# Expert down projection: both weight parts in one 512-column matmul, halves added on the way out of PSUM

## The chip, the cores and the metric

The kernel runs on one core of a Trainium2 chip. The metric is the device time of one execution in microseconds; smaller is better. Three runs of the kernel before gave 782.05, 783.87 and 785.30 us. The trace is that of one further execution with the hardware profiler on.

## The reference

One transformer layer: a layer norm modulated by a vector c, causal attention with 16 heads over 2048 tokens of width 256, and a mixture of 8 experts. The part that the change touches is the experts:

```python
C = _capacity(T, E)                      # 320 slots for each of E = 8 experts
...
dispatch_data = jnp.einsum('tec,th->ech', sec_mask_f, tokens)
h = jnp.einsum('ech,ehi->eci', dispatch_data, wi)        # 320 x 256 by 256 x 1024
h = jax.nn.gelu(h, approximate=False)
expert_out = jnp.einsum('eci,eih->ech', h, wo)           # 320 x 1024 by 1024 x 256
ans = jnp.einsum('tec,ech->th', combine_weights, expert_out)
...
x = x + gb * _L0_ffn_ref(h, ...)
```

Each token goes to one expert at most, so the result row of a slot is the token's row of x plus gb times its gate probability times the expert's row.

## The kernel before

Attention comes first and takes some 600 us; then tokens are ranked, scattered into slot rows in HBM (`slot_rows`, 320 for each expert, each with the row of x, the normalised row, the probability and the token's number) and read back by expert into `slots_sb`. The change touches only the expert stage behind that.

**Tiles.** An expert's 320 slots are CT3 = 3 row tiles of 128, 128 and 64 rows. Its inner width of 1024 is cut into IT = 8 tiles of 128. The engines walk through n = 0 to 63 (expert e = n // 8, inner tile it = n % 8).

**Split numbers.** Matmuls take 4-byte operands in the format fp32r, which keeps fewer bits than float32. To keep the precision every operand is held as a high part (rounded) and a low part (the rest): `w_split[e % 2][:, 0]` and `[:, 1]` for the weights, `acts[:, n % 3, 0]` and `[:, 1]` for the activations. A product is made of three terms, low x high, high x low and high x high (PAIRS, L1401).

**TensorE** (L1439 to L1448). `up(n)` makes six matmuls of 320 columns into bank n % 3 (L1413). At the first inner tile of an expert, `turn_slots` transposes the next expert's slots (L1396). Then `down_to(n - 2)` makes, for each of the three row tiles, three matmuls of 256 columns (L1430): the activations are the stationary operand, the weights stream, and the result adds up over the eight inner tiles in columns 0 to 255 of the bank of that row tile (banks 3, 4, 5; each holds 512 columns of float32). So down_to of an expert's last inner tile runs behind up of the next expert's second one, and the next expert's first down_to waits for `down_read` of each row tile, the mark that DVE has read the bank (L1428).

**ACT** waits for `up_done`, makes Gelu twice, once rounded into acts (L862) and once in full into act_raw (L865), and in between casts the next expert's weights (L837, inner tiles 2 to 5) and turns its slots (L843, inner tile 0).

**DVE** makes the low part of acts (L1139), the low part of the next expert's weights (L1098) and slots (L1106, L1109). At the second inner tile of an expert it calls `finish_rows` for the one before: for each row tile bank times probability times the gate row (L1120). `add_rows` adds the token's row of x (L1127), one row tile at the second, one at the seventh and one at the eighth inner tile. Behind the last expert both run at once for all three.

**POOL** waits for each row tile (L730) and scatters it to `out` by an indirect DMA (L731). The instructions of each engine run in order. `link` on POOL (L645) gives an instruction a mark and makes the engine's next instruction wait for it.

**SP** loads the weights and slots of later experts; slots of expert e reuse those of e - 4 once their rows are stored (L628).

Of the kernel before, what the change touches and what calls it, by code (L numbers as in the profile page):

```python
# [21 lines left out]
F32 = mybir.dt.float32  # L22
# [4 lines left out]
ALU = mybir.AluOpType  # L27
ACT = mybir.ActivationFunctionType
AX = mybir.AxisListType

P = 128
D = 256
# [17 lines left out]
E = 8  # L50
I = 1024
IT = I // P
# [3 lines left out]
CT3 = -(-CAP // P)  # L56
CAPW = CT3 * P
LAST_ROWS = CAP - (CT3 - 1) * P
BIAS_FROM = (NG - 2) * NB
DOWN_LAG = 2  # L60
TAIL_TILES = (NB - 1) * TB
# [214 lines left out]
def layer(nc, x, w_qk, b_qk, w_v, w_o, b_rows, w_gate, w_in, w_down, c_col, w_mod, out):  # L276
# [13 lines left out]
    with ExitStack() as ctx:  # L290
        def sem(name):
            return ctx.enter_context(nc.semaphore(name))

        def sb(name, shape, dt):
            return ctx.enter_context(nc.sbuf_tensor(name, shape, dt))
# [5 lines left out]
        DOWN_BANKS, SLOT_BANKS = (3, 4, 5), (6, 7)  # L301
# [83 lines left out]
        SR = 4  # L385
# [4 lines left out]
        AR = 3  # L390
        acts = sb("acts", [P, AR, 2, CAPW], F32R)
        down = sb("down", [P, 2, CT3, D], F32)


        loaded_c = sem("loaded_c")
# [79 lines left out]
        act_used = sem("act_used")  # L475
        down_done = sem("down_done")
        down_read = sem("down_read")
        rows_ready = sem("rows_ready")
        kept_stored = sem("kept_stored")
        rows_stored = [sem(f"rows_stored{r}") for r in range(2)]  # L480
# [48 lines left out]
        def rows_of(st):  # L529
            return min(P, CAP - st * P)  # L530
# [111 lines left out]
        def _(pool):  # L642
# [84 lines left out]
            for e in range(E):  # L727
                for st in range(CT3):
                    rows = rows_of(st)
                    pool.wait_ge(rows_ready, CT3 * e + st + 1)  # L730
                    pool.indirect_dma_start(  # L731
                        out=out, out_offset=bass.IndirectOffsetOnAxis(
                            ap=slots_sb[0:rows, e % SR, st, ROW - 1:ROW].bitcast(U32), axis=0),
                        in_=down[0:rows, e % 2, st, :], in_offset=None, bounds_check=S - 1, oob_is_err=False)\
                        .then_inc(rows_stored[e % 2], 16)
# [4 lines left out]
        def _(act):  # L740
# [98 lines left out]
            def split_slots(e):  # L839

                for ft in range(DT):
                    act.wait_ge(slots_turned, e * DT + ft + 1)
                    act.activation(slotT[:, e % 2, 0, ft, :], bank[SLOT_BANKS[ft]][:, 0:CAP], ACT.Identity,  # L843
                                   bias=mod_col[:, 2, ft:ft + 1], scale=mod_col[:, 3, ft:ft + 1]).then_inc(slotT_high, 1)


            act.activation(c_tmp[0:1, 2, 0:1], c_tmp[0:1, 0, 0:1], ACT.Gelu)

            act.wait_ge(max_scored, units_before[-1])
# [3 lines left out]
            for n in range(E * IT):  # L853
                e, it = divmod(n, IT)
                act.wait_ge(up_done, n + 1)
                if n >= AR:

                    m = n - AR
                    act.wait_ge(act_used, (IT - 1) * (m // IT) + min(m % IT + 1, IT - 1))
                    if m % IT == IT - 1:  # L860
                        act.wait_ge(down_done, CT3 * (m // IT + 1))
                act.activation(acts[:, n % AR, 0, 0:CAP], bank[n % 3][:, 0:CAP], ACT.Gelu)  # L862
                if n >= 2:
                    act.wait_ge(act_ready, n - 1)
                act.activation(act_raw[:, n % 2, :], bank[n % 3][:, 0:CAP], ACT.Gelu).then_inc(gelu_done, 1)  # L865
                if e + 1 < E and 2 <= it < 2 + CH:
                    split_weights(e + 1, it - 2)
                if e + 1 < E and it == 0:
                    split_slots(e + 1)

        @block.vector
        def _(dve):
# [239 lines left out]
            def finish_rows(e):  # L1112

                if e >= 2:
                    dve.wait_ge(rows_stored[e % 2], 16 * CT3 * (e // 2))
                for st in range(CT3):
                    k = CT3 * e + st
                    r = slice(0, rows_of(st))
                    dve.wait_ge(down_done, k + 1)
                    dve.scalar_tensor_tensor(out=down[r, e % 2, st, :], in0=bank[DOWN_BANKS[st]][r, 0:D],  # L1120
                                             scalar=slots_sb[r, e % SR, st, 2 * D:2 * D + 1], in1=gates[r, 1, :],
                                             op0=ALU.mult, op1=ALU.mult).then_inc(down_read, 1)

            def add_rows(e, st):
                r = slice(0, rows_of(st))
                dve.wait_ge(down_read, CT3 * e + st + 1)
                dve.tensor_tensor(down[r, e % 2, st, :], down[r, e % 2, st, :], slots_sb[r, e % SR, st, 0:D],  # L1127
                                  ALU.add).then_inc(rows_ready, 1)

            ADD_AT = (DOWN_LAG - 1, IT - 2, IT - 1)  # L1130
            dve.memset(acts[:, :, :, CAP:CAPW].bitcast(F32), 0.0).then_inc(pads_zeroed, 1)
            for c in range(CH):
                split_weights(0, c)
# [2 lines left out]
            for n in range(E * IT):  # L1136
                e, it = divmod(n, IT)
                dve.wait_ge(gelu_done, n + 1)
                dve.tensor_tensor(acts[:, n % AR, 1, 0:CAP], act_raw[:, n % 2, :], acts[:, n % AR, 0, 0:CAP].bitcast(F32),  # L1139
                                  ALU.subtract).then_inc(act_ready, 1)  # L1140
                if it == DOWN_LAG - 1 and e >= 1:
                    finish_rows(e - 1)
                if it in ADD_AT and e >= 1:
                    add_rows(e - 1, ADD_AT.index(it))
                if e + 1 < E:
                    if 2 <= it < 2 + CH:
                        split_weights(e + 1, it - 2)
                    if it in (0, IT - 2):
                        split_slots(e + 1, 0 if it == 0 else 1)
            finish_rows(E - 1)  # L1150
            for st in range(CT3):
                add_rows(E - 1, st)

        @block.tensor
        def _(pe):
# [262 lines left out]
            def down_to(n):  # L1418
                e, it = divmod(n, IT)
                if it == 0:  # L1420
                    pe.wait_ge(w_ready, CH * (e + 1))
                if n == 0:
                    pe.wait_ge(pads_zeroed, 1)
                pe.wait_ge(act_ready, n + 1)
                col = DT * I + it * D
                for st in range(CT3):
                    if it == 0 and e >= 1:
                        pe.wait_ge(down_read, CT3 * (e - 1) + st + 1)  # L1428
                    for i, (a, b) in enumerate(PAIRS):
                        mm = pe.matmul(bank[DOWN_BANKS[st]][:, 0:D], acts[:, n % AR, a, st * P:(st + 1) * P],  # L1430
                                       w_split[e % 2][:, b, col:col + D], start=(it == 0 and i == 0),
                                       stop=(it == IT - 1 and i == len(PAIRS) - 1))
                    if it == IT - 1:
                        mm.then_inc(down_done, 1)
                if it < IT - 1:
                    mm.then_inc(act_used, 1)
# [45 lines left out]
```

## Time and profile before

| | |
|---|---|
| Three runs, us | 782.05, 783.87 (median), 785.30 |
| Span of the profiled execution, us | 782.6 |
| Instructions | 12208 |
| PE busy | 689.1 us, 88% |
| PE weight loads busy | 367.2 us, 47% |
| DVE busy | 561.1 us, 72% |
| ACT busy | 459.5 us, 59% |
| POOL busy | 133.9 us, 17% |
| Mean granted TensorE clock | 0.943 of 2.4 GHz |

The shares are means over the whole span, and the attention has other limits than the experts. PE's busy time overlaps: a matmul's record covers its way through the array as well, so the distance from one start to the next tells what it costs, not its own duration. "Idle before" in a row is the time that the engine stood still ahead of that instruction, with what released it.

### The profile page before, as it was taken

The numbers are of one execution on the slowest core, as the hardware profiler recorded it, in microseconds if no ns is written. First come the engines' busy times: TensorE is split into PE (matmuls) and PEld (weight loads), VectorE is DVE, ScalarE is ACT, GpSimd is POOL, SyncE is SP. The second block draws the span as 40 slices with busy tenths as digits, with TensorE's granted clock in tenths as the row PEclk, the third lists the DMA queues.
The fourth block names the chain that finished last, engine by engine and source line by source line (L and its number), as shares of the span: only waits on it lengthen the run. The fifth ranks groups of instructions, "written<-read, shape, count | busy, mean of one in ns | idle before, by whom it ended". The sixth has DMA issues, their size and how long they took to land.

```text
span 782.6 us, 12208 instructions
## 1 busy us (share of the span) xinstructions
PE 689.1 (88%) x4290; PEld 367.2 (47%) x4290; DVE 561.1 (72%) x1467; ACT 459.5 (59%) x962; POOL 133.9 (17%) x194
## 2 busy tenths in 40 slices
PE   4686989999999998999999999989996279999994
PEld 3564534432323343323332323242543269999994
DVE  7754778788888787988888898960435437777762
ACT  1422445566676667766677676657783336656551
POOL 6000222220001132003310201100105300121122
PEclk9869889999999999999999999999999559999998
DMA  7436126630006033005900006000004283455200
GB/s 243 109 76 144 41 57 147 162 68 14 2 0 162 1 81 81 2 1 124 308 1 1 1 1 214 1 28 1 28 28 162 90 234 115 155 182 201 92 23 17
DMA packets 42111, 66.53 MB, mean 85 GB/s; under 512 B 3822, under 2 KB 31985, under 8 KB 41466
## 3 DMA queue, kind: packets, MB, share of 16 engines
q1 hardware_dynamic: 39746, 59.44, 27.3%
q0 software_dynamic: 2304, 6.31, 2.2%
q8 instruction: 34, 0.56, 0.3%
q14 instruction: 27, 0.22, 0.1%
HBM read 39.36 MB, written 26.78 MB: 85 GB/s over the span
## 4 chain that ended last, share of the span: by engine, by line
PE 74%; DVE 10%; ACT 8%; issue 4%; DMA 2%; POOL 1%; SPq 0%; DVEq 0%; POOLq 0%; ACTq 0%
PE bank L1245 17%; PE bank L1295 15%; PE bank L1325 14%; PE bank L1430 9%; PE bank L1413 8%; ACT probs L802 4%; PE bank L1187 3%; DVE chunk_max L1049 2%; PE bank L1350 2%; PE bank L1216 1%; PE bank L1396 1%; ACT qk_sb L751 1%; PE bank L1373 1%; PE bank L1228 1%; DVE stats L907 1%
## 5 line engine op out<-in xcount | busy, mean ns | idle before, releaser
L802 ACT ACTIVATE probs<-bank 128x512 f32<-128x512 f32 (+3 forms) x640 | 298.3, 537 | 124.1 <-PE bank L1325 123.0
L1049 DVE TENSOR_REDUCE chunk_max<-bank 128x1 f32<-128x512 f32 x384 | 250.7, 685 | 36.9 <-PE bank L1295 35.9
L1325 PE MATMUL bank<-stacks 104*128 104x512 bf16 (+3 forms) x640 | 195.4, 356 | 13.5 <-ACT probs L802 10.1
L1295 PE MATMUL bank<-stacks 96*128 96x512 bf16 (+3 forms) x640 | 197.7, 359 | 7.9 <-DVE chunk_max L1049 3.2
L1245 PE MATMUL bank<-probs,v_sb 128*32 128x512 f32 (+3 forms) x1280 | 151.6, 546 | 0.1
L1055 DVE CUSTOM_DVE_ANT_0 masked<-bank,causal 128x128 bf16<-128x128 f32 (+3 forms) x256 | 120.7, 484 | 15.4 <-PE bank L1295 14.6
L1295 PEld LDWEIGHTS bank<-stacks 96*128 96x128 bf16 x640 | 56.0, 98 | 160.0 <-DVE chunk_max L1049 79.4
L698 POOL TENSOR_SCALAR_AFFINE_SELECT probs<-probs 128x512 f32<-128x512 f32 x64 | 40.6, 635 | 397.4 <-ACT probs L802 397.4
L1325 PEld LDWEIGHTS bank<-stacks 104*128 104x128 bf16 x640 | 62.2, 100 | 98.7 <-ACT probs L802 65.6
L1430 PE MATMUL bank<-w_split,acts 128*128 128x256 f32 x576 | 79.9, 284 | 0.0
L1430 PEld LDWEIGHTS bank<-w_split,acts 128*128 128x128 f32 x576 | 74.5, 190 | 1.5 <-issue 0.8
L1413 PE MATMUL bank<-slotT,w_split 128*128 128x320 f32 x384 | 70.0, 320 | 2.1 <-DVE slotT L1109 2.1
L1413 PEld LDWEIGHTS bank<-slotT,w_split 128*128 128x128 f32 x384 | 59.5, 196 | 3.1 <-issue 2.3
L862 ACT ACTIVATE acts<-bank 128x320 fp32r<-128x320 f32 x64 | 28.0, 438 | 55.4 <-PE bank L1413 55.4
L1139 DVE TENSOR_TENSOR acts<-act_raw,acts 128x320 fp32r<-128x320 f32 x64 | 31.4, 490 | 33.6 <-ACT act_raw L865 33.6
L1187 PEld LDWEIGHTS bank<-hT,w_qk_sb 128*128 128x128 f32 x256 | 40.7, 219 | 13.8 <-issue 9.1
L1098 DVE TENSOR_TENSOR w_split<-w_raw,w_split 128x1024 fp32r<-128x1024 f32 x32 | 38.9, 1224 | 10.6 <-ACT w_split L837 10.6
L731 POOL DMA_INDIRECT out<-down,slots_sb x24 | 23.6, 984 | 132.0 <-DVE down L1127 127.2
L1187 PE MATMUL bank<-hT,w_qk_sb 128*128 128x128 f32 x256 | 43.7, 309 | 2.7 <-ACT hT L771 2.7
L1245 PEld LDWEIGHTS bank<-probs,v_sb 128*32 128x32 f32 x1280 | 25.4, 108 | 44.0 <-issue 27.6
L751 ACT ACTIVATE qk_sb<-bank,b_qk_sb,qk_scale 128x512 f32<-128x512 f32 x16 | 12.4, 777 | 43.2 <-PE bank L1187 43.2
L837 ACT CAST w_split<-w_raw 128x1024 fp32r<-128x1024 f32 x32 | 33.3, 1049 | 0.0
(140 smaller groups left out, 533.6 us busy)
## 6 DMA issues: line engine op xcount, KB each, us to landing
stacks<-qk_rows SPq DMA_DIRECT2D x6, 1536.0 KB, 12.4
w_raw<-w_in SPq DMA_DIRECT2D x8, 1024.0 KB, 5.0
w_raw<-w_down SPq DMA_DIRECT2D x8, 1024.0 KB, 8.0
qk_rows<-part SPq DMA_DIRECT2D x32, 192.0 KB, 2.9
slot_rows<-empty SPq DMA_DIRECT2D x1, 5140.0 KB, 28.9
slots_sb<-slot_rows SPq DMA_DIRECT2D x8, 514.0 KB, 4.0
qk_rows<-part SPq DMA_DIRECT2D x32, 128.0 KB, 2.4
stacks<-qk_rows SPq DMA_DIRECT2D x8, 384.0 KB, 4.5
```

Of the source, the lines that this page charges most:

```text
L698: pool.affine_select(out=d, in_=d, compare_op=ALU.is_ge, fill=0.0, base=0, pattern=[[0, HG], [1, P]], channel_multiplier=-1).then_inc(diag ...
L802: act.activation(probs[:, s % 3, h, 0:width], bank[SCORE_BANKS[u % 3]][:, 0:width], ACT.Exp)\
L837: act.copy(chunk(w_split[e % 2][:, 0, :], c), chunk(w_raw[:, e % 2, :], c)).then_inc(w_high, 1)
L1049: dve.tensor_reduce(to, src[:, 0:QB], AX.X, ALU.max).then_inc(max_read, 1)
L1055: dve.tensor_tensor_reduce(out=masked[:, u % 3, 0:width], in0=src[:, 0:width], in1=causal[:, QB - width:QB], scale=1.0, scalar=NEG, op0=AL ...
L1098: dve.tensor_tensor(chunk(w_split[e % 2][:, 1, :], c), chunk(w_raw[:, e % 2, :], c), chunk(w_split[e % 2][:, 0, :], c).bitcast(F32), ALU.s ...
L1187: mm = pe.matmul(bank[MISC_BANK][:, at:at + width], w_qk_sb[:, k, g * P:(g + 1) * P], hT[:, k, b * QB + at:b * QB + at + width], start=(k ...
L1245: mm = pe.matmul(bank[VALUE_BANK][CT * h:CT * (h + 1), lo:QB], v_sb[:, kt, g * HG + h, :], probs[:, s % 3, h, 0:QB - lo], start=first, sto ...
L1295: pe.matmul(bank[MAX_BANKS[u % 3]][:, 0:width], stack(g, 0)[0:KR, h, q0:q0 + P], stack(g, 1)[0:KR, h, c * QB:c * QB + width], start=True, ...
L1325: pe.matmul(bank[SCORE_BANKS[u % 3]][:, 0:QB - lo], stack(g, 1)[0:KR + MR, h, kt * P:(kt + 1) * P], stack(g, 0)[0:KR + MR, h, b * QB + lo: ...
L1413: mm = pe.matmul(bank[n % 3][:, 0:CAP], w_split[e % 2][:, a, col:col + P], slotT[:, e % 2, b, k, :], start=(i == 0 and k == 0), stop=(i == ...
L1430: mm = pe.matmul(bank[DOWN_BANKS[st]][:, 0:D], acts[:, n % AR, a, st * P:(st + 1) * P], w_split[e % 2][:, b, col:col + D], start=(it == 0 ...
```

## The change

In `down_to` the high activations now stream the high and the low weights as one matmul of 512 columns: its result fills the whole bank, high x high in columns 0 to 255 and high x low in 256 to 511. The second matmul, low activations by high weights, adds to columns 256 to 511. The last row tile uses 66 stationary columns, not 128. The two halves of a bank must now be added. ACT does the first step in a new function `scale_low`: columns 256 to 511 times probability into `low_part`. It stands behind the Gelus of the second inner tile, and behind the loop for the last expert. DVE's `finish_rows` waits for it and makes columns 0 to 255 times probability plus low_part. The gate product that this displaces becomes the former `add_rows`, now `gate_rows`, and the addition of x's row moves to POOL, in front of each scatter, through `link`.

```diff
+LAST_COLS = LAST_ROWS + 2
...
+        low_part = sb("low_part", [P, CT3, D], F32)
...
                     pool.wait_ge(rows_ready, CT3 * e + st + 1)
+                    link(pool.tensor_tensor(down[0:rows, e % 2, st, :], down[0:rows, e % 2, st, :],
+                                            slots_sb[0:rows, e % SR, st, 0:D], ALU.add))
                     pool.indirect_dma_start(
...
+            def scale_low(e):
+
+                for st in range(CT3):
+                    k = CT3 * e + st
+                    r = slice(0, rows_of(st))
+                    act.wait_ge(down_done, k + 1)
+                    if e >= 1:
+                        act.wait_ge(down_read, k + 1 - CT3)
+                    act.activation(low_part[r, st, :], bank[DOWN_BANKS[st]][r, D:2 * D], ACT.Copy,
+                                   scale=slots_sb[r, e % SR, st, 2 * D:2 * D + 1]).then_inc(low_scaled, 1)
...
+                if it == DOWN_LAG - 1 and e >= 1:
+                    scale_low(e - 1)
                 if e + 1 < E and 2 <= it < 2 + CH:
                     split_weights(e + 1, it - 2)
...
+            scale_low(E - 1)
...
-                    dve.wait_ge(down_done, k + 1)
+                    dve.wait_ge(low_scaled, k + 1)
                     dve.scalar_tensor_tensor(out=down[r, e % 2, st, :], in0=bank[DOWN_BANKS[st]][r, 0:D],
-                                             scalar=slots_sb[r, e % SR, st, 2 * D:2 * D + 1], in1=gates[r, 1, :],
-                                             op0=ALU.mult, op1=ALU.mult).then_inc(down_read, 1)
-
-            def add_rows(e, st):
+                                             scalar=slots_sb[r, e % SR, st, 2 * D:2 * D + 1], in1=low_part[r, st, :],
+                                             op0=ALU.mult, op1=ALU.add).then_inc(down_read, 1)
+
+            def gate_rows(e, st):
...
-                dve.tensor_tensor(down[r, e % 2, st, :], down[r, e % 2, st, :], slots_sb[r, e % SR, st, 0:D],
-                                  ALU.add).then_inc(rows_ready, 1)
+                dve.tensor_tensor(down[r, e % 2, st, :], down[r, e % 2, st, :], gates[r, 1, :],
+                                  ALU.mult).then_inc(rows_ready, 1)
...
-                    for i, (a, b) in enumerate(PAIRS):
-                        mm = pe.matmul(bank[DOWN_BANKS[st]][:, 0:D], acts[:, n % AR, a, st * P:(st + 1) * P],
-                                       w_split[e % 2][:, b, col:col + D], start=(it == 0 and i == 0),
-                                       stop=(it == IT - 1 and i == len(PAIRS) - 1))
+                    at = st * P
+                    cols = P if st < CT3 - 1 else LAST_COLS
+                    out = bank[DOWN_BANKS[st]][0:cols, :]
+
+                    pe.matmul(out.rearrange("p (a d) -> p a d", a=2), acts[:, n % AR, 0, at:at + cols],
+                              w_split[e % 2][:, :, col:col + D], start=it == 0, stop=True, skip_group_check=True)
+                    mm = pe.matmul(out[:, D:2 * D], acts[:, n % AR, 1, at:at + cols],
+                                   w_split[e % 2][:, 0, col:col + D], start=False, stop=True, skip_group_check=True)
```

## Rows read from the trace of the kernel before

**Rows 1.** The page: busy tenths in 40 slices of 19.6 us, TensorE and its granted clock

```profile
PE   4686989999999998999999999989996279999994
...
PEclk9869889999999999999999999999999559999998
```

**Rows 2.** Busy time by stretch: length, then PE, PEld, DVE, ACT, POOL, clock, DMA

```profile
645.00:772.00 127.00, 127.00 (x948) 122.31 (x947) 88.77 (x156) 76.39 (x158) 20.14 (x21) 1.00 0.37 119
```

**Rows 3.** The chain that ended last, in the expert stage: start, us, what

```profile
704.23 0.99 PE bank L1396 x6
...
707.38 1.06 PE bank L1430 x9
708.45 0.89 PE bank L1413 x6
```

**Rows 4.** Waits from 640 to 783 us: in total, times, the longest

```profile
POOL out L731 <- DVE down L1127: 127.2, 16, 37.8
ACT acts L862 <- PE bank L1413: 50.7, 62, 1.4
```

**Rows 5.** Timeline of the end: start, us, what [idle before <-releaser]

```profile
769.10 3.33 PE L1430 MATMUL bank<-w_split,acts 128*128 128x256 f32 x27
...
770.51 0.41 DVE L1127 TENSOR_TENSOR down<-down,slots_sb 64x256 f32<-64x256 f32 x1
771.71 0.91 POOL L731 DMA_INDIRECT out<-down,slots_sb  x1 [0.96 <-DVE down L1127]
771.84 1.26 DVE L1120 SCALAR_TENSOR_TENSOR down<-bank,slots_sb,gates 128x256 f32<-128x256 f32 x3 [0.92 <-PE bank L1430]
773.02 1.08 DVE L1127 TENSOR_TENSOR down<-down,slots_sb 128x256 f32<-128x256 f32 x3
774.22 0.97 POOL L731 DMA_INDIRECT out<-down,slots_sb  x1 [1.60 <-DVE down L1127]
775.50 0.97 POOL L731 DMA_INDIRECT out<-down,slots_sb  x1 [0.31 <-issue]
776.78 0.91 POOL L731 DMA_INDIRECT out<-down,slots_sb  x1 [0.30 <-issue]
```

**Rows 6.** Groups by line from 600 us on: count | busy us, mean ns | idle before

```profile
L1430 PE MATMUL bank<-w_split,acts 128*128 128x256 f32 x576 | 79.9, 284 | 0.0
L1430 PEld LDWEIGHTS bank<-w_split,acts 128*128 128x128 f32 x576 | 74.5, 190 | 1.5 <-issue 0.8
...
L824 ACT COPY rest<-bank 128x256 f32<-128x256 f32 x4 | 1.5, 372 | 8.7 <-PE bank L1361 8.7
...
L847 ACT ACT_TABLE_LOAD x1 | 1.3, 1283 | 0.0
```

**Rows 7.** The chain at the stage's start, with the clock still at 1.2 GHz

```profile
640.34 1.92 PE bank L1430 x9
```

**Rows 8.** Timeline of PE in the attention: start, us, what

```profile
299.81 0.38 PE L1325 MATMUL bank<-stacks 104*128 104x512 bf16 x1
300.02 0.33 PE L1295 MATMUL bank<-stacks 96*128 96x384 bf16 x1
...
301.02 0.39 PE L1325 MATMUL bank<-stacks 104*128 104x512 bf16 x1
301.34 1.07 PE L1245 MATMUL bank<-probs,v_sb 128*32 128x512 f32 x8
```

**Rows 9.** Timelines of ACT and of DVE at an expert's boundary

```profile
707.75 0.43 ACT L865 ACTIVATE act_raw<-bank 128x320 f32<-128x320 f32 x1
709.37 0.44 ACT L862 ACTIVATE acts<-bank 128x320 fp32r<-128x320 f32 x1 [1.18 <-PE bank L1413]
709.70 0.43 ACT L865 ACTIVATE act_raw<-bank 128x320 f32<-128x320 f32 x1
...
708.63 1.25 DVE L1120 SCALAR_TENSOR_TENSOR down<-bank,slots_sb,gates 128x256 f32<-128x256 f32 x3
```

**Rows 10.** POOL's additions in the attention stage: ns min/median/max

```profile
L711 POOL TENSOR_TENSOR token<-token,product x16: 635/687/747, 367.6 to 447.0; 128x256 f32<-128x256 f32 x16
```

More of the change, by code:

```diff
@@ L477, in layer @@
         down_read = sem("down_read")
+        low_scaled = sem("low_scaled")
         rows_ready = sem("rows_ready")
@@ L1118, in finish_rows @@
                     r = slice(0, rows_of(st))
-                    dve.wait_ge(down_done, k + 1)
+                    dve.wait_ge(low_scaled, k + 1)
                     dve.scalar_tensor_tensor(out=down[r, e % 2, st, :], in0=bank[DOWN_BANKS[st]][r, 0:D],
-                                             scalar=slots_sb[r, e % SR, st, 2 * D:2 * D + 1], in1=gates[r, 1, :],
-                                             op0=ALU.mult, op1=ALU.mult).then_inc(down_read, 1)
-            def add_rows(e, st):
+                                             scalar=slots_sb[r, e % SR, st, 2 * D:2 * D + 1], in1=low_part[r, st, :],
+                                             op0=ALU.mult, op1=ALU.add).then_inc(down_read, 1)
+            def gate_rows(e, st):
                 r = slice(0, rows_of(st))
                 dve.wait_ge(down_read, CT3 * e + st + 1)
-                dve.tensor_tensor(down[r, e % 2, st, :], down[r, e % 2, st, :], slots_sb[r, e % SR, st, 0:D],
-                                  ALU.add).then_inc(rows_ready, 1)
-            ADD_AT = (DOWN_LAG - 1, IT - 2, IT - 1)
+                dve.tensor_tensor(down[r, e % 2, st, :], down[r, e % 2, st, :], gates[r, 1, :],
+                                  ALU.mult).then_inc(rows_ready, 1)
+            GATE_AT = (DOWN_LAG - 1, IT - 2, IT - 1)
             dve.memset(acts[:, :, :, CAP:CAPW].bitcast(F32), 0.0).then_inc(pads_zeroed, 1)
@@ L1142, in _ @@
                     finish_rows(e - 1)
-                if it in ADD_AT and e >= 1:
-                    add_rows(e - 1, ADD_AT.index(it))
+                if it in GATE_AT and e >= 1:
+                    gate_rows(e - 1, GATE_AT.index(it))
                 if e + 1 < E:
@@ L1151, in _ @@
             for st in range(CT3):
-                add_rows(E - 1, st)
+                gate_rows(E - 1, st)
         @block.tensor
```

## The prediction

> **What bounds the kernel now.** I read the page first: its slices show TensorE at nine tenths or more in six of the last eight, with the granted clock at nine tenths in seven of them [rows 1]. The expert stage is this last sixth of the span, and only it holds changed code, so I asked for the busy time of each engine in that stretch [rows 2]: from 645 to 772 us PE is busy for all of 127 us at a granted clock of 1.00 (2.4 GHz), DVE for 88.8, ACT for 76.4, POOL for 20.1. Then the chain that ended last, inside the stage [rows 3]: it alternates between L1430 (9 matmuls in 1.06 us) and L1413 (6 in 0.89 us), with nearly 60 such pieces of each in the stage, and nothing else stands between them except 6 transposes for each expert. So the stage lasts as long as TensorE's stream. The waits say the same from the other side [rows 4]: ACT waits 50.7 us for L1413, and POOL 127.2 us for DVE's rows. Work added to ACT, DVE or POOL inside the stage is free as long as it fits in these holes; behind the last matmul nothing hides it.
>
> Last comes that end [rows 5]: the last 27 matmuls end at 772.43 us, DVE's three products and three additions run from 771.84 to 774.10, and then POOL's three scatters start at 774.22, 775.50 and 776.78. The third is over at 777.69, and 4.9 us of landing and draining end the span of 782.6 us.
>
> **The change, part by part.**
>
> *Matmuls of the down projection.* For each of 64 calls and 3 row tiles, three matmuls of 256 columns become one of 512 and one of 256. Streamed columns stay 768, so the arithmetic offers nothing: 576 matmuls and as many weight loads [rows 6] become 384, and only what a matmul costs beyond its columns can go. What is that? 1.055 us over 9 (the pieces are 1.05 or 1.06) is 117.2 ns for 256 columns; 0.885 over 6 (0.88 or 0.89) is 147.5 ns for 320 [rows 3]. At 2.4 GHz, 256 columns are 106.7 ns and 320 are 133.3, so the excess is 10.5 and 14.2 ns. It grows with the columns: 0.458 and 0.461 ns per column, nearly one rate. At the lower clock it is absent: 9 in 1.92 us are 213.3 ns each, exactly 256 columns at 1.2 GHz [rows 7]. The 512-column bf16 matmul of the attention also shows almost none: it starts at 299.81 and the next one at 300.02 [rows 8]. This looks like a rate at which 4-byte data are delivered, not like a price per instruction or per load. The 512-column form is not in the trace in 4 bytes, so I bound it: at the rate of the 256-column one it takes 234.4 ns, and the edit gives 0; through the two points as a line, 238, which is +4 ns x 192 = +0.8 us; if the excess is one per instruction, 224, which is -10.5 x 192 = -2.0 us; at bf16's pace, 215, -19.4 x 192 = -3.7 us. I take -0.5 us, a quarter of the way from the equal rate to the price per instruction, since the two points lie much nearer to the rate. Its operand is now two runs of 256 elements, w_split's high and low part; no row prices that, and if each jump costs 10 ns (my guess at a bound, about the excess of one matmul) it is +1.9 us.
>
> The Trainium skill (TensorE: Matmul & The Clock Gate, section Back-to-back issue gap) gives a gap of N/2.4 + 2.5 ns for a warm matmul. By it the edit would save one 2.5 ns in each of 192 places, an estimate of 0.5 us. The measured 117.2 ns for 256 columns is 8 ns above that rule's 109.2, so the rule does not describe these 4-byte streams.
>
> *66 instead of 128 weight columns in the last row tile.* It streams as many columns. Its load is shorter, but loads already lie beside matmuls (L1430's group idles 1.5 us in all before its loads) [rows 6]. Zero, unless the array is switched to another shape (a rival, below).
>
> *ACT's new scale_low, 3 activations of 128x256 per expert.* The nearest row is L824, 372 ns, of the same form [rows 6]. At an expert's boundary ACT starts L865 at 707.75 and is free at 708.1, and its next work waits for L1413 until 709.37 [rows 9]. Three at 372 are 1.1 us; these overlap by about 0.1 us, as L862 and L865 do (0.33 us apart for 0.44 each), which makes 0.9. The first can start at once, because row tile 0 is done a third of the way into the call that began at 707.38 [rows 3]. The three end near 709.0, with 0.3 us left. DVE reaches its products only at 708.63, when the first low part has been ready since 708.5; the following ones come every 0.3 us against DVE's 0.4. So DVE's order and times stay, PE's first matmul of the next expert still finds its bank read, and this costs nothing in the stage. If the cover were gone, each 0.1 us on DVE's first product would delay PE seven times. The activation is a Copy; the stage's only table load is the one at its start [rows 6], though copies of weights run on ACT throughout.
>
> *DVE.* The product takes another operand, the addition becomes a product with the gate: same forms, three in 1.26 and three in 1.08 us at the end [rows 5]. Zero.
>
> *POOL's addition before each scatter, with a wait for itself.* 24 additions of 128x256. POOL has the same form in the attention stage: 635 to 747, median 687 ns [rows 10]. In the stage, 21 of them lie in POOL's idle time [rows 4], and the rows they finish are due only by a transfer many microseconds later: zero. In the tail all three stand in line.
>
> *The tail, step by step.* ACT's first activation must end before DVE's first product: 0.37 + 0.06 for the handover (L1413 ends at 709.34 and ACT starts at 709.37, and a semaphore wait of its own stands in each) = 0.43 us [rows 3, 9]. Then POOL's first addition, 0.69 + 0.10 of start and handover (an estimate, three times that 0.03): 0.79. Then each further scatter: today the pitch is 1.28 us (775.50 - 774.22), since the preparation of the next scatter runs beside the one before. The wait put behind the addition forbids that. From the end of DVE's addition (770.92) to the scatter's start (771.71) there are 0.79 us [rows 5]; so the new pitch is 0.10 + 0.69 + 0.79 + 0.97 = 2.55 us, or 1.27 more, twice: 2.54. The tail grows by 0.43 + 0.79 + 2.54 = 3.8 us. Low end: the preparation stays hidden in both later scatters (each only +0.79): 2.8. High end: a start of 0.31 us behind a scatter, as the present gap, and 0.6 us of blocking (below): 4.8.
>
> **Sum.** 782.6 - 0.5 + 3.8 = 785.9 us for the profiled execution, that is +3.3. The median shown is 783.9, 1.3 us above that span, inside the 782.05 to 785.3 of its runs; the forecast for the median is 787.2.
>
> **Rivals.**
>
> A, the merge pays after all: the 512-column matmul runs as its bf16 counterpart. -3.7 + 3.8 = +0.1: 784.0. For it: the bf16 row [rows 8]. Against: the near constant rate of the two 4-byte forms.
>
> B, per-instruction excess: -2.0 + 3.8 = +1.8, 785.7. The trace cannot exclude it.
>
> C, slower clearly: the 66-column weights count as another shape of the array and their loads can no longer run beside the matmul before. The trace prices such a switch: L1325, 512 columns, starts at 301.02, and L1245, whose weights have 32 columns, at 301.34, 0.32 us instead of 0.21 [rows 8]. Two switches a call x 64 x 0.1 = 13 us: 800. With the tail's 3.8 us already spent, it takes the kernel past 3.9 us slower from about 5 ns per switch on (0.6 us over 128). Against it: 104 and 96 rows follow each other at full pace in the same rows, so a partial size above half the array does not switch.
>
> D, POOL's addition is held off by DVE: then the first would start only after DVE's third product with the gate, about 0.6 us later, +3.9 and 787.8 in all. The Trainium skill (SBUF — State Buffer, section Who interferes with whom) calls the port pair of VectorE and GpSimd an exclusive lock, which speaks against this change. POOL's additions ran in 635 to 747 ns beside a DVE that worked on PSUM, so no row here shows the conflict.
>
> E, a clearly faster kernel would need the merge to save over 7.7 us, twice the bf16 bound. Only a drift of the clock's rise at the start of the stage could add it.
>
> **How the numbers follow.** A measurement of this kernel can tell about 0.5%, 3.9 us, from no change. Main forecast 45%, A 10%, B 18%, C 5%, D 14% (with small costs of the two runs in it), E and the unforeseen 8%. The main case reaches from 786.5 to 788.3, so about a third of it is past 787.8; D about two thirds; C wholly. Slower 0.34, same 0.62, faster 0.04. The range, 783.3 to 790.5, goes from A's value less some scatter of the runs to +1.9 +4.8 over the median; it leaves C out.
>
> **What would show it.** Starts of L1430's new forms: 234 ns apart behind the 512-column form and 117 behind the other; 215 would be A, 224 B, over 300 around the 66-column form C. The nine-matmul piece of 1.06 us becomes a six-matmul piece of 1.05. ACT's idle before L862 at the boundary shrinks from 1.18 to about 0.3 us. POOL's last three scatters stand 2.5 us apart, and the time from the last matmul's end to the span's end grows from 10.2 to 14 us. The prediction is wrong if PE waits for down_read at the boundaries, or if the scatters stay 1.3 us apart.

## The result

| | median, us | runs, us | ratio to before, 95% interval |
|---|---|---|---|
| before | 782.96 | 781.72 to 785.30 (4) | |
| changed | 792.63 | 788.38 to 794.27 (4) | 1.009 (1.0046 to 1.0133) |
| changed, again (below) | 788.79 | 788.20 to 793.95 (12) | 1.0063 (1.0037 to 1.0088) |

The kernel became slower, by 4 to 10 us. Each ratio is to the runs of the kernel before that were made beside it (for the last row their median was 784.58). The forecast for the median was 787.2 with a range up to 790.5: the direction was right, the first median lies above the range (its ratio of 1.009 on 782.96 us gives 790.0), and the second, with three times as many runs, lies inside. The profiled execution of the changed kernel has a span of 789.4 us, 6.8 more than before's 782.6.

Where are these 6.8 us? The page of the changed kernel looks like that of before [rows 1], except for the clock in the first slices and POOL at the end. POOL before, then the changed kernel:

```profile
POOL 6000222220001132003310201100105300121122
```

```profile
span 789.4 us, 11893 instructions
...
POOL 6000212220001132002320201100105201332324
PEclk9967789999999999999999999999999569999997
```

*The tail.* Timeline of POOL, then of ACT and DVE, around the end of the last matmuls; the answer to [rows 5]:

```profile
776.14 0.92 POOL L736 DMA_INDIRECT out<-down,slots_sb  x1 [0.79 <-POOL down L734]
777.07 0.74 POOL L734 TENSOR_TENSOR down<-down,slots_sb 128x256 f32<-128x256 f32 x1
778.60 0.99 POOL L736 DMA_INDIRECT out<-down,slots_sb  x1 [0.80 <-POOL down L734]
779.62 0.75 POOL L734 TENSOR_TENSOR down<-down,slots_sb 128x256 f32<-128x256 f32 x1
781.16 0.99 POOL L736 DMA_INDIRECT out<-down,slots_sb  x1 [0.80 <-POOL down L734]
782.17 0.66 POOL L734 TENSOR_TENSOR down<-down,slots_sb 64x256 f32<-64x256 f32 x1
783.62 0.92 POOL L736 DMA_INDIRECT out<-down,slots_sb  x1 [0.80 <-POOL down L734]
...
774.80 1.19 ACT L860 ACTIVATE low_part<-bank,slots_sb 128x256 f32<-128x256 f32 x3 [1.68 <-PE bank L1454]
775.38 1.26 DVE L1139 SCALAR_TENSOR_TENSOR down<-bank,slots_sb,low_part 128x256 f32<-128x256 f32 x3 [1.36 <-ACT low_part L860]
776.56 1.52 DVE L1146 TENSOR_TENSOR down<-down,gates 128x256 f32<-128x256 f32 x3
```

The last three scatters stand 2.56 and 2.46 us apart (1.28 and 1.28 before): 0.99 scatter, 0.75 addition (0.66 for 64 rows), 0.80 from its end to the next scatter. The last matmul ends at 775.47, so the *tail*, the time from there to the end of the span, is 13.9 us against 10.1: +3.8.

The chain that ended last shows what the tail hangs on:

```profile
772.14 0.64 POOL down L734
772.83 0.73 issue
773.57 0.99 POOL out L736
774.58 0.77 POOL down L734
775.41 0.73 issue
776.14 0.92 POOL out L736
777.07 0.75 POOL down L734
```

From 772.14 us on, 3.3 us ahead of the last matmul's end, it is POOL's queue alone: the last two row tiles of the seventh expert, then the three of the eighth. DVE's first product with the gate ends at 776.97, and POOL's scatter of the seventh expert frees it at 777.05: the way over ACT and DVE is as long as POOL's queue within 0.1 us, and a little shorter.

*The stage.* The chain of one expert; the answer to [rows 3]:

```profile
705.98 1.11 PE bank L1432 x6
707.09 0.99 PE bank L1415 x6
708.09 0.43 PE bank L1452
...
709.33 0.88 PE bank L1432 x6
...
711.26 0.89 PE bank L1432 x6
712.14 0.44 PE bank L1452
...
713.40 0.88 PE bank L1432 x6
...
715.33 0.89 PE bank L1432 x6
```

From here on I give the *period*: the time from the first matmul of one up (L1432) to that of the next. An undisturbed period is 1.933 us (715.33 - 713.40), 1.940 before; at the third inner tile it is 2.14 (713.40 - 711.26; 2.12 before), at the last one 2.09 and 2.19 in turn (2.05 before). These two waits stood in the chain of before too, as pieces of 1.23 and 1.08 us among those of 1.06 and 0.89:

```profile
709.33 1.23 PE bank L1430 x9
...
720.26 1.08 PE bank L1413 x6
```

The experts 1 to 7 took 116.3 us up to the last up's start before, and 116.5 here: the small gain of the merge went into longer waits.

*Ahead of the stage.* The rest, 4.2 us at the first up (633.26 against 637.46), less 1.3 us in the first expert, whose first half runs before the clock has risen. No instruction there was changed. The two traces run within about 1 us of each other up to 67 us; then the changed kernel's lies 4.5 us behind from 77 us on, and about as much up to the experts. Busy time and granted clock (the last but two columns) from 60 to 80 us, first before, then changed:

```profile
60.00:80.00 20.00, 12.82 (x70) 9.61 (x70) 8.65 (x24) 4.77 (x6) 0.00 (x0) 0.89 0.56 131
```

```profile
60.00:80.00 20.00, 14.04 (x56) 11.17 (x56) 5.88 (x14) 4.00 (x4) 0.00 (x0) 0.74 0.55 131
```

The clock was at 2.4 GHz until 75.7 us in the one and fell to 1.2 GHz at 66.8 us in the other. Whether the change causes that was the first question.

### The profile page after: what moved, and what is told of

It reads as the page before. It is cut to its first block, busy times and chain, and to the rows that moved or that the text cites. A ratio compares the mean times of both kernels' runs of the same rounds, so it can differ in the third digit from the quotient of the medians.

```text
span 789.4 us, 11893 instructions
## 1 busy us (share of the span) xinstructions
PE 692.0 (88%) x4098; PEld 355.7 (45%) x4098; DVE 562.5 (71%) x1467; ACT 468.2 (59%) x986; POOL 153.8 (19%) x218
## 4 chain that ended last, share of the span: by engine, by line
PE 74%; DVE 9%; ACT 8%; issue 4%; DMA 2%; POOL 1%; SPq 0%; POOLq 0%; DVEq 0%; ACTq 0%
PE bank L1264 17%; PE bank L1314 15%; PE bank L1344 14%; PE bank L1432 8%; PE bank L1452 6%; ACT probs L807 4%; PE bank L1206 4%; PE bank L1454 3%; DVE chunk_max L1068 2%; PE bank L1369 2%; PE bank L1235 1%; ACT qk_sb L756 1%; PE bank L1415 1%; PE bank L1392 1%; PE bank L1247 1%
## 5 line engine op out<-in xcount | busy, mean ns | idle before, releaser
L1344 PE MATMUL bank<-stacks 104*128 104x512 bf16 (+3 forms) x640 | 195.4, 356 | 13.5 <-ACT probs L807 10.1
L1432 PE MATMUL bank<-slotT,w_split 128*128 128x320 f32 x384 | 69.5, 318 | 2.4 <-DVE slotT L1128 2.1
L1452 PE MATMUL bank<-w_split,acts 128*128 128x512 f32 (+1 forms) x192 | 70.9, 399 | 0.0
L1432 PEld LDWEIGHTS bank<-slotT,w_split 128*128 128x128 f32 x384 | 59.3, 194 | 9.9 <-issue 4.6
L1454 PE MATMUL bank<-w_split,acts 128*128 128x256 f32 (+1 forms) x192 | 53.8, 280 | 0.0
L734 POOL TENSOR_TENSOR down<-down,slots_sb 128x256 f32<-128x256 f32 (+1 forms) x24 | 18.0, 749 | 95.3 <-DVE down L1146 95.1
L1452 PEld LDWEIGHTS bank<-w_split,acts 128*128 128x128 f32 (+1 forms) x192 | 32.7, 170 | 7.5 <-issue 1.3
```

The lines of the kernel that those rows point to most:

```text
L1344: pe.matmul(bank[SCORE_BANKS[u % 3]][:, 0:QB - lo], stack(g, 1)[0:KR + MR, h, kt * P:(kt + 1) * P], stack(g, 0)[0:KR + MR, h, b * QB + lo: ...
L1432: mm = pe.matmul(bank[n % 3][:, 0:CAP], w_split[e % 2][:, a, col:col + P], slotT[:, e % 2, b, k, :], start=(i == 0 and k == 0), stop=(i == ...
L1452: pe.matmul(out.rearrange("p (a d) -> p a d", a=2), acts[:, n % AR, 0, at:at + cols], w_split[e % 2][:, :, col:col + D], start=it == 0, st ...
L1454: mm = pe.matmul(out[:, D:2 * D], acts[:, n % AR, 1, at:at + cols], w_split[e % 2][:, 0, col:col + D], start=False, stop=True, skip_group_ ...
```

## The experiments

### The prologue: chance, or the new declarations?

```diff
+        low_part = sb("low_part", [P, CT3, D], F32)
...
+        low_scaled = sem("low_scaled")
```

> The kernel before with the new tile and the new semaphore declared and nothing else. Question: the changed kernel's profiled execution was 4.5 us behind from 78 us on, long before any changed instruction, with PE at 1.2 GHz from 66.8 us on, where before it had 2.4 GHz until 75.7 us. Theory P (phase: it is chance from run to run where the clock's changes fall against the start): this kernel equals the kernel before, ratio 0.998 to 1.002, and its runs spread over 781 to 786 us. Theory D (the declarations move something): it is 4 to 5 us slower, ratio 1.005 or more, and its profile too loses 4.5 us between 67 and 78 us.

Measured: 1.0008 (0.9979 to 1.0038), 780.4 us in the profile. The declarations do nothing that can be seen. Beside it the changed kernel ran again.

> The changed kernel once more, on the same chip as the three beside it. Theory P (chance in the prologue): ratio 1.004 to 1.006, with some of its runs below 787 us. Theory D or another cause inside the changed program: ratio 1.009 to 1.012 again, and PE at 1.2 GHz from about 67 to 77 us in its profile.

Measured: 788.79 us against 784.58, ratio 1.0063 (1.0037 to 1.0088), profile 787.5 us with its first up at 634.33 and not 637.46. The ratio is between the two expectations and its interval covers the first; but Theory P had also asked for some runs below 787 us, and the lowest of the 12 is 788.20. Over all profiles taken here the first up starts anywhere from 632.5 to 641.0 us, whatever is changed behind it: 632.5 with the bare declarations, 632.5 and 640.5 in two kernels of this study that leave out the merge, 632.7 and 641.0 in two that have it. So, as far as these traces show, the 4.2 us ahead of the stage belong to that trace and not to the change. The same scatter would explain how wide the runs of the kernel before lie (780.6 to 790.9 in 32 runs), which isn't shown, as most runs have no trace. Tail and stage together make 4.0 us of the 4.9 that the ratio gives; a rest of that size is within its interval. The tail was 13.9 us again.

### Who makes the tail?

The addition goes back to DVE:

```diff
-                    link(pool.tensor_tensor(down[0:rows, e % 2, st, :], down[0:rows, e % 2, st, :],
-                                            slots_sb[0:rows, e % SR, st, 0:D], ALU.add))
...
-                dve.tensor_tensor(down[r, e % 2, st, :], down[r, e % 2, st, :], gates[r, 1, :],
-                                  ALU.mult).then_inc(rows_ready, 1)
+                link(dve.tensor_tensor(down[r, e % 2, st, :], down[r, e % 2, st, :], gates[r, 1, :], ALU.mult))
+                dve.tensor_tensor(down[r, e % 2, st, :], down[r, e % 2, st, :], slots_sb[r, e % SR, st, 0:D],
+                                  ALU.add).then_inc(rows_ready, 1)
```

> The changed kernel with the addition of x's row given back to DVE, behind its product with the gate; POOL only scatters. Theory Q (POOL's additions make the tail longer): the last three scatters stand 1.28 us apart and not 2.56, and from the last matmul's end to the span's end it takes 11.1 us (10.2 of before, 0.43 for ACT, 0.4 for one more DVE operation) and not 13.9; so 2.8 us less than the changed kernel. It also says that PE's waits at the expert's last inner tile (period 2.09 to 2.19 us, 2.05 before) go back to about 2.05, since no POOL addition holds up DVE. Rival R (ACT's new step and the longer chain, not POOL, make the tail): 13.5 us or more stay. If the prologue's loss is chance, the ratio to before is 1.001; if it belongs to the changed program, 1.007.

The tail did nearly what Theory Q says: 11.3 us for 11.1, 2.6 less than in the changed kernel, with the last scatters 1.48 and 1.28 us apart. The whole did not: 788.79 us, ratio 1.0041 (1.0013 to 1.007), the same median as the changed kernel beside it. The chain shows where the gain went, and DVE's timeline what stood in front:

```profile
763.04 0.43 issue
763.47 1.13 PE bank L1431 x6
```

```profile
761.45 0.42 DVE L1144 TENSOR_TENSOR down<-down,gates 128x256 f32<-128x256 f32 x1
761.90 0.42 DVE L1145 TENSOR_TENSOR down<-down,slots_sb 128x256 f32<-128x256 f32 x1
762.24 0.60 DVE L1123 TENSOR_SCALAR slotT_raw<-bank,mod_col 128x320 f32<-128x320 f32 x1
762.88 0.49 DVE L1126 TENSOR_TENSOR slotT<-slotT_raw,slotT 128x320 fp32r<-128x320 f32 x1
```

The period of each expert's last inner tile is now 2.52 us and not 2.09 to 2.19. At the tile before, DVE makes the product and the addition of row tile 1 ahead of the low part of the next expert's slots (L1126), on which PE's next up waits. PE stands still for 0.43 us there, 6 times. Experts 1 to 7 take 118.8 us against 116.5 in the changed kernel: 2.3 us, most of the 2.6 that the tail had won. I had expected a shorter wait there. DVE's "idle" share says nothing on this: the wait is for one operation in its queue.

The other way round, POOL's addition alone on the kernel before:

```diff
-                    dve.scalar_tensor_tensor(out=down[r, e % 2, st, :], in0=bank[DOWN_BANKS[st]][r, 0:D],
-                                             scalar=slots_sb[r, e % SR, st, 2 * D:2 * D + 1], in1=gates[r, 1, :],
-                                             op0=ALU.mult, op1=ALU.mult).then_inc(down_read, 1)
+                    dve.tensor_scalar(down[r, e % 2, st, :], bank[DOWN_BANKS[st]][r, 0:D],
+                                      slots_sb[r, e % SR, st, 2 * D:2 * D + 1], None, ALU.mult).then_inc(down_read, 1)
...
-                dve.tensor_tensor(down[r, e % 2, st, :], down[r, e % 2, st, :], slots_sb[r, e % SR, st, 0:D],
-                                  ALU.add).then_inc(rows_ready, 1)
+                dve.tensor_tensor(down[r, e % 2, st, :], down[r, e % 2, st, :], gates[r, 1, :],
+                                  ALU.mult).then_inc(rows_ready, 1)
```

> The kernel before with one part of the change alone: DVE multiplies by the probability, then by the gate, and POOL adds x's row ahead of each scatter. PE and ACT as before. Theory Q: the tail grows by 0.8 + 2 x 1.27 = 3.3 us, to 13.5 us from the last matmul's end; ratio 1.004. Rival R: the tail grows by less than 1.5 us. The prologue: under chance as before; under a cause in POOL's added instructions, 4 us slower in it, ratio 1.009.

Measured: 789.72 us, ratio 1.006 (1.0021 to 1.0099), tail 14.2 us (+4.1), experts 1 to 7 in 116.85 us (+0.5). This one edit costs what the whole change costs. The tail is longer than expected and longer than with ACT's step, because here POOL is still at the seventh expert's last row tile when the first row tile of the eighth is ready:

```profile
771.47 1.15 POOL L733 DMA_INDIRECT out<-down,slots_sb  x1 [0.79 <-POOL down L731]
772.63 0.83 POOL L731 TENSOR_TENSOR down<-down,slots_sb 128x256 f32<-128x256 f32 x1
```

The scatter frees POOL at 772.62 and the addition starts at once, though DVE's row has been ready since 771.82. As in the changed kernel, the tail is POOL's queue from the seventh expert on. So ACT's step, which this kernel doesn't have, is no term of the changed kernel's tail: it lies beside POOL's queue.

### Does POOL's addition hold up DVE?

In the pool_add_only kernel, DVE has as many operations as before, and yet the last period went from 2.05 to 2.08 and 2.18 in turn. The changed kernel, with a fill in place of the addition:

```diff
-                    link(pool.tensor_tensor(down[0:rows, e % 2, st, :], down[0:rows, e % 2, st, :],
-                                            slots_sb[0:rows, e % SR, st, 0:D], ALU.add))
+                    link(pool.memset(scratch[0:rows, :], 0.0))
```

> The changed kernel, but POOL fills a tile of its own with zeros where it added x's row (so x's row is missing from the experts' output): the same queue and wait, but POOL reads nothing from SBUF. Theory L (POOL's addition and DVE's operations with two inputs from SBUF can't run together: the shared ports that the Trainium skill names in SBUF — State Buffer, Who interferes with whom): DVE's last product with the gate takes 0.41 us and not 0.85, and the period of an expert's last inner tile is 2.05 us, not 2.09 to 2.19. Rival M (it is POOL's scatter, or the later marks, that slow them): 0.85 and 2.09 to 2.19 stay. The tail shortens only by what a fill is shorter than an addition; the scatters stay some 2.2 to 2.6 us apart, since the wait behind it stays.

Measured, timeline of DVE in the tail, then POOL's first fill there:

```profile
779.61 1.08 DVE L1146 TENSOR_TENSOR down<-down,gates 128x256 f32<-128x256 f32 x3
...
780.07 0.52 POOL L735 MEMSET scratch<- 128x512 f32 x1 [0.29 <-DVE down L1146]
```

Theory L: the three products take 1.08 us and not 1.52, though POOL's fill runs beside them, and the last period is 2.06 us in every expert. An addition of POOL that reads from SBUF and a DVE operation with two inputs there did not run together; a fill did not disturb. The fill also writes to another tile and is 0.2 us shorter; these two were not told apart from the reading. In the stage that costs 0.03 to 0.13 us an expert, 0.5 us in all, for which the prediction had zero. In the tail DVE's third product was the loser (0.85 us), not POOL's first addition, so it cost nothing. With the Trainium skill's rule (SBUF — State Buffer, section Who interferes with whom), an exclusive lock on shared ports when a VectorE operation with two SBUF inputs meets a GpSimd operation that reads SBUF and not one that only writes it, these rows agree: 1.52 us beside the addition, 1.08 beside the fill. The scatters stayed 2.31 us apart (the fill takes 0.53), as the wait behind it stayed.

### What limits a 4-byte stream?

First the two runs of the 512-column operand, replaced by one of the high weights alone:

```diff
-                    pe.matmul(out.rearrange("p (a d) -> p a d", a=2), acts[:, n % AR, 0, at:at + cols],
-                              w_split[e % 2][:, :, col:col + D], start=it == 0, stop=True, skip_group_check=True)
+                    run = min(col, 2 * DT * I - 2 * D)
+                    pe.matmul(out, acts[:, n % AR, 0, at:at + cols],
+                              w_split[e % 2][:, 0, run:run + 2 * D], start=it == 0, stop=True, skip_group_check=True)
```

> The merged matmul's 512 streamed columns are taken from one contiguous run of the high weights and not from two runs (so the products are others than the reference's); everything else as in the kernel with the additions on DVE. Theory S (4-byte data stream at one rate, whatever the pattern): start to start behind the 512-column form stays 231 to 232 ns. Rival J (the jump between the two runs costs): 220 to 228 ns.

Measured: 232 ns (median) behind the 512-column form, period 1.933 us. The jump costs nothing that can be seen. Then constant bf16 operands of the same shape:

```diff
+                    pe.matmul(out, flat[:, 0:cols], flat[:, 0:2 * D], start=it == 0, stop=True, skip_group_check=True)
+                    mm = pe.matmul(out[:, D:2 * D], flat[:, 0:cols], flat[:, 0:D], start=False, stop=True, skip_group_check=True)
```

> The kernel with the additions on DVE, but the down projection's matmuls take both operands from a constant bf16 tile (so the products are not the reference's), of the same forms: 512 and 256 columns, 128 and 66 stationary columns. Theory S (the excess over the column count comes from 4-byte operands): start to start 215 to 217 ns behind the 512-column form and 108 to 110 behind the other, period of an inner tile 1.933 - 3 x 0.024 = 1.86 us. Rival (it comes from writing to PSUM or from the stage's other engines): 231 and 117 stay.

Timelines of PE, first the changed kernel, then this one:

```profile
701.26 0.39 PE L1452 MATMUL bank<-w_split,acts 128*128 128x512 f32 x1
701.49 0.28 PE L1454 MATMUL bank<-w_split,acts 128*128 128x256 f32 x1
701.61 0.39 PE L1452 MATMUL bank<-w_split,acts 128*66 128x512 f32 x1
```

```profile
701.54 0.38 PE L1453 MATMUL bank<-flat 128*128 128x512 bf16 x1
701.75 0.27 PE L1454 MATMUL bank<-flat 128*128 128x256 bf16 x1
701.86 0.38 PE L1453 MATMUL bank<-flat 128*66 128x512 bf16 x1
```

0.23 + 0.12 us against 0.21 + 0.11; the medians are 232 and 117 ns against 217 and 109. In the same place of the same stage, 7% is the price of 4-byte operands. The run changes the stationary operand's type too, so it doesn't tell the load from the stream. The period fell to 1.88 us only, where 1.86 was expected (the rest is not explained), and the last one rose to 2.71: with PE ahead of it, the wait for DVE grew.

### Does the array change shape at 64 columns?

```diff
-LAST_COLS = LAST_ROWS + 2
+LAST_COLS = LAST_ROWS
```

> The last row tile with 64 stationary columns and not 66, on the kernel with the additions on DVE. Theory T (up to half the array's columns is another shape of the array, and its load can't run beside the matmul before it): each change of shape costs about 90 ns as between L1325 and L1245 in the attention, two for each call, so an inner tile's period grows from 1.933 to about 2.11 us, and the kernel by 11 us. Rival: the period stays within 0.02 us of 1.933.

Measured: period 1.927 us, 6 ns shorter than with 66. Theory T falls, and with it the mechanism of my rival C: 64 stationary columns load beside the matmul before them here like 128.

### The waits that remain

The kernel before in a new order on DVE (ADD_AT as before):

```diff
+                if it == DOWN_LAG - 1 and e >= 1:
+                    finish_rows(e - 1)
                 dve.wait_ge(gelu_done, n + 1)
                 ...
-                if it == DOWN_LAG - 1 and e >= 1:
-                    finish_rows(e - 1)
-                if it in ADD_AT and e >= 1:
-                    add_rows(e - 1, ADD_AT.index(it))
                 if e + 1 < E:
                     ...
                         split_slots(e + 1, 0 if it == 0 else 1)
-            finish_rows(E - 1)
+                if it in ADD_AT and e >= 1:
+                    add_rows(e - 1, ADD_AT.index(it))
             for st in range(CT3):
+                finish_rows(E - 1, (st,))
                 add_rows(E - 1, st)
```

> The kernel before with DVE's order alone changed, at three places: at an expert's second inner tile its products come ahead of the low part of the activations, at the seventh and eighth the addition comes behind the slots' low part, and behind the last expert product and addition alternate by row tile. Theory W (the stage's remaining stalls of PE are waits for DVE at two inner tiles of each expert: periods of 2.12 and 2.05 us against 1.94): they fall to 1.94 to 1.98, 7 x (0.15 + 0.10) = 1.7 us, and the first scatter of the end starts 0.75 us earlier; 2.4 us in all, ratio 0.997. Rival (those stalls belong to PE's own switch from one waited matmul to another): the periods stay, only the 0.75 us of the tail is won, ratio 0.999.

Measured: 783.95 us against 785.86, ratio 0.9959 (0.9926 to 0.9991), tail 9.5 us. The chain of an expert no longer has a disturbed piece but the transposes:

```profile
755.87 1.06 PE bank L1430 x9
756.93 0.88 PE bank L1413 x6
757.81 1.06 PE bank L1430 x9
758.87 0.88 PE bank L1413 x6
```

All periods but those with the transposes are 1.940 us: Theory W. Experts 1 to 7 take 113.9 us, 2.4 less than before where 1.7 was expected, as the period with the transposes fell too, from 3.22 to 3.13. The same order with the merge:

> The merged matmul with ACT's step and all three row operations on DVE, in the new order. Against the same kernel in the old order (last inner tile's period 2.52 us, 2.13 at the third, tail 11.3 us): Theory W says 2.52 falls to 1.93 to 1.97, 2.13 to about 2.0, as DVE then has only ACT's first activation ahead of it, and the tail to 10.6 us: 7 x 0.55 + 7 x 0.13 + 0.7 = 5.4 us less. Against the kernel before: 0.45 us from 64 periods of 1.933 and not 1.940, and 1.6 from the waits, less 0.4 of tail: ratio 0.998. Rival: ACT's step now sets DVE's first product, and PE waits longer at the third inner tile (2.2 us or more): ratio 1.000 or above. Against the reordered kernel without the merge it can win 0.5 us at most.

Measured: 784.01 us, ratio 0.9987 (0.996 to 1.0014), tail 10.5 us. The last period fell from 2.52 to 1.934; the third inner tile's stayed at 2.07 to 2.15, where 2.0 was expected. ACT shows why:

```profile
741.66 0.43 ACT L879 ACTIVATE act_raw<-bank 128x320 f32<-128x320 f32 x1
741.98 1.18 ACT L858 ACTIVATE low_part<-bank,slots_sb 128x256 f32<-128x256 f32 x3
743.26 0.44 ACT L876 ACTIVATE acts<-bank 128x320 fp32r<-128x320 f32 x1
```

Its three activations begin only behind both Gelus and take 1.18 us, 0.48 each and not the 0.37 of L824, a copy without a scale. So ACT's step 0 goes between the Gelus:

```diff
                 act.activation(acts[:, n % AR, 0, 0:CAP], bank[n % 3][:, 0:CAP], ACT.Gelu)
+                if it == DOWN_LAG - 1 and e >= 1:
+                    scale_low(e - 1, (0,))
...
-                    scale_low(e - 1)
+                    scale_low(e - 1, (1, 2))
```

> The merged and reordered kernel, where the third inner tile still has a period of 2.07 to 2.15 us against 1.94 without the merge. Here ACT scales row tile 0 between the two Gelus and not behind both. Theory A (ACT's first step comes too late for DVE's first product, and that for PE): the period falls to 1.93 to 1.97 and the kernel by 7 x 0.18 = 1.3 us, to a ratio of 0.996 to 0.998 to the kernel before. Rival (PE's event wait itself costs it): no change.

Measured: 782.96 us against 785.61, ratio 0.9968 (0.9945 to 0.9991); the period is 2.04 to 2.06, so half of the 0.2 us went, where Theory A expected nearly all. The waits tell what the rest is:

```profile
PEld bank L1453 <- DVE down L1139: 1.1, 7, 0.2
```

PE now waits at the second row tile and not at the first: ACT's second step, still behind the second Gelu, ends at 740.84, DVE's second product runs from 740.88 to 741.36, and PE's load starts at 741.42. So in this trace the rest is ACT's and DVE's too, and not PE's own. Without the merge the reordered kernel has a ratio of 0.9959, with it 0.9968; the intervals overlap. By the traces the merge adds nothing to the reordered kernel: an expert takes 16.76 us with it and 16.72 without, and the tail is 1.0 us longer.

## Why the prediction was right, and where it was not

**The bound** was read rightly in the main: the merge, which shortens PE's stream, and the steps on ACT, DVE and POOL each counted only where the chain ran through them. But the prediction took the chain of the stage for nothing but pieces of 1.06 and 0.89 us with the transposes. It passed over the longer ones: at two inner tiles of each expert PE already waited before (periods of 2.12 and 2.05 us against 1.94), and those are the places where work on another engine isn't free. By its own sign of being wrong, a wait of PE for down_read at the boundary, it was wrong there: 0.2 us an expert, most of it there before.

**The merge.** The prediction took -0.5 us, from 4-byte rows that grow almost in proportion to the columns. Measured: 232 + 117 ns a row tile for 3 x 117.2, a period 7 ns shorter, 0.45 us for 64 periods. The bf16 end (-3.7) was far off, and so was the price per instruction (-2.0); the line through the two points was wrong in sign. The 2.5 ns per matmul of the Trainium skill (TensorE: Matmul & The Clock Gate, section Back-to-back issue gap), three for each period, is 7.5 ns, an estimate that agrees with the 7 ns measured. The page gives its formula for an isolated matmul, which the prediction left out, and the times here lie above it: 117 ns where it gives 109.2, and 232 where it gives 215.8.

**The tail.** Predicted +3.8, measured +3.8. Step by step: DVE's first product came 0.50 us later for 0.43 (ACT's activation takes 0.48 us and not 0.37), the first addition took 0.84 with its handover for 0.79, and the two pitches grew by 2.46 together for 2.54. The pitch is the prediction's mechanism, and it holds. That the sum comes out is in part luck: the tail isn't that sum but POOL's queue, which began with the seventh expert, and the way over ACT that was added up happens to be as long within 0.1 us. Without ACT's step the addition alone made 4.1 us in the kernel before.

**"This costs nothing in the stage"** is the step that failed. On ACT two margins were smaller than taken: the three steps end 0.1 us ahead of the next Gelu and not 0.3, which still costs nothing; and the first one ends only at 711.38, so that DVE's product starts at 711.48, where 0.1 us was to be spare. The period there grew by some 0.02 us. POOL's additions were put at zero as they lie in its idle time; but they held DVE's two-input operations up, the period behind grew by 0.03 to 0.13 us, and one of those operations is what PE waits for. Together 0.6 us, which ate the merge's gain. Rival D named the lock, and put it in the tail, where it cost nothing; it acted in the stage. A sum of 3.8 in the tail and 0.2 in the stage comes to 4.0 us, where 3.3 was forecast; the second comparison measured 4.2 us (4.9 by the ratio).

**The range and the chances.** The first median, 792.6, lies above 790.5. The two traces put 4.2 us of the 6.8 ahead of the stage, where nothing was changed. The prediction took the runs shown (782 to 785) as the kernel's scatter; 32 runs lay between 780.6 and 790.9. With that scatter (a standard deviation of 2.8 us) two means of four runs can differ by 4 us by chance, an estimate. "Within 0.5%" had 0.62 and came out wrong: at 0.63% and 0.9% both comparisons are above, the second with an interval from 0.37%.

**Rivals.** A (215 ns) and B (224) fell with the 232 ns. C fell with the run at 64 columns. A shape change had been read from L1325 to L1245, whose weights have 32 columns; that price doesn't carry over to 64.

## What to carry to other kernels

A stage bound by one engine still has waits of a tenth of a microsecond on single operations of the others; look which operation in the idle engine's queue stands ahead of the awaited one, and put the awaited one first. Here that brought 0.4% without a new instruction, while moving work to an idle engine lost 0.6%. A wait put between two instructions of POOL cost nothing by itself in mid-stage; in the tail it set the pace, from the seventh expert's rows on, as the queue could no longer prepare the next scatter ahead.

## What the runs showed of the hardware that I had not expected

- A load of 64 stationary columns hides beside the matmul before it: period 1.927 us against 1.933 with 66.
- In POOL's queue, 0.80 us lie between an awaited operation's end and the start of the indirect scatter behind it, and 0.31 us between two scatters that wait for nothing.
- An activation of 128x256 from PSUM takes 0.48 us with a scale per partition from SBUF, and a copy of the same size 0.37.
- With the same instructions ahead of it, the first up started between 632.5 and 641.0 us. Part of that is there by 80 us, where the granted clock's levels fall at other times from trace to trace; the rest comes later.
- POOL's addition and DVE's third product with the gate, both from SBUF, did not run together: 0.85 us for the product beside it, 0.41 without.
